# Applying the layer norms on ScalarE instead of VectorE, with new order tables, in a one-core macaron block

## The chip, the cores and the metric

The kernel runs on one core of a Trainium2 chip. The metric is device time in microseconds (us) for the whole program, from the first to the last instruction and what lies around them. The engines of a core each run their own queue of instructions in order and meet at semaphores: TensorE (PE, with its weight loads shown apart as PEld), VectorE (DVE), ScalarE (ACT), GpSimd (POOL) and SyncE (SP), which here issues every DMA.

## What is computed

The input is x of shape (8, 1024, 256), float32. A feed-forward step at half weight, an attention step and the same feed-forward step again are added to x, each on a layer norm of x:

```python
def _layernorm(x, axis=-1, eps=1e-05):
    m = jnp.mean(x, axis=axis, keepdims=True)
    v = jnp.var(x, axis=axis, keepdims=True)
    return (x - m) / jnp.sqrt(v + eps)

x = L0_attn_x
x = x + 0.5 * _L0_ffn_ref(_layernorm(x, axis=-1), ...)
x = x + _L0_attn_ref(_layernorm(x, axis=-1), ...)
x = x + 0.5 * _L0_ffn_ref(_layernorm(x, axis=-1), ...)
```

The feed-forward step is a 256x256 matrix with a bias, and eight low-rank experts of rank 16, of which each row takes the two with the largest gates. The attention step has 16 heads with causal softmax; keys and values come from a latent of 64 that is normed by its root mean square, queries from a latent of 128, and 32 of a head's 48 key and query columns are rotated.

## The kernel before, in words

Attention is worked in 32 quads: a quad g is four heads of one of the eight batches, so four quads make a batch. The work beside attention is cut into 32 jobs of 512 rows (four tiles of 128 rows by 256 columns): 16 jobs before attention (first feed-forward step, second layer norm, latents) and 16 after it (output projection, feed-forward step). Nearly all jobs run one after the other in lane 0, whose rows lie in the tile xa and whose normed rows lie in xn; job 1 and the last job run in lane 1, whose tiles are cut out of the tile probs and so bear that name in the trace.

The order of every engine's steps is written out by hand as a table of letters, ORDER: a head, a stretch for one batch that is repeated four times, and a tail. Each letter stands for the next step of one kind. On TensorE, S is one score tile (two matmuls, lines 643 and 645, into one of two banks of st_b), X one tile for the row maxima (line 673, into one of two banks of mx_b), V the probabilities times the values (line 661), P a projection (lines 694 to 700), T and F turns of keys and queries and of the maxima (lines 712, 679), J and j a piece of a job. On ScalarE, E is the exponential of a score tile (line 733), C and H copies for P and T (lines 742, 743, 755). On VectorE, M is a row maximum (lines 820 and 823), L the second half of a turn (line 864). Because each engine takes its queue strictly in that order, a step that is not ready holds up all that stands behind it.

A layer norm goes like this. VectorE takes the statistics of the four tiles (line 885) and joins them into mean and variance, mv (line 892). GpSimd adds the epsilon to the variance (line 1026, into ve) and raises it to the power -0.5 (line 1028, into rs). VectorE then makes xn of xa, four instructions of 128x256 a layer norm in two steps of two (line 906), and the semaphore normed lets TensorE transpose xn (line 587) and GpSimd add the bias to xa (line 1035). A job before attention has two layer norms and a job after attention has one: 48 layer norms, 192 instructions of line 906.

Behind that, TensorE's job pieces are named tr0, tr1 (transposes, line 587), low0, low1 (line 594), gated_tr (599), y0, y1 (605, 607), tr20, tr21 (587), qc (613), kv (619), kvt (625) and, for a job after attention, first wo0 and wo1 (line 576), the output projection. wo0 needs the tile aoc, a load of 512 KB of the attention's results (line 507). It stands in SyncE's queue behind the load of the job's rows xa (line 491), which in turn stands behind the store of the job before (line 513) or, when that job was one before attention, behind the store of its latents (lines 519, 520). Those wait for the copy out of kvt.

The row maxima go back into the scores as an extra row: after the turn F (line 679) VectorE writes the tile shift (line 838), SyncE stores it to DRAM (539) and loads it back as a row of st (543), and the first score of that half of the quad waits for it.

## Time and profile before

| what | us |
|---|---|
| median of 3 runs | 2131.92 |
| lowest and highest of the 3 | 2131.22, 2135.18 |
| the profiled execution | 2139.53 |
| its span, first to last instruction | 2137.8 |

Busy times of the profiled execution over its span: PE 2013.1 us (94%), DVE 1675.6 (78%), ACT 1263.9 (59%), POOL 972.0 (45%); the mean granted clock of TensorE is 0.985 of full speed. In the profile a matmul's end is modelled, so TensorE can be shown as busy while it in fact waits for a short time between two matmuls: the distance from one start to the next says more than the duration. Idle time shown for an engine is attributed to what released it.

### The profile page before, as it was taken

How to read it: one execution, taken by the hardware profiler on the slowest of the kernel's cores; microseconds unless marked ns; L12 is line 12 of the kernel's file. 1: busy time of each engine (PE TensorE's matmuls, PEld its weight loads, DVE VectorE, ACT ScalarE, POOL GpSimd, SP SyncE). 2: the span in 40 equal slices, each digit the busy share in tenths (PEclk: the TensorE clock that was granted, in tenths of full speed). 3: DMA queues.
4: the chain of work that ended last, by engine and by line, in shares of the span. 5: the costliest groups of instructions: out<-in, count | busy, mean ns of one | idle time of the engine just before them, and what ended most of it. 6: DMA issues, size and time to landing. Idle time of an engine off the chain costs nothing.

```text
span 2137.8 us, 38517 instructions
## 1 busy us (share of the span) xinstructions
PE 2013.1 (94%) x13248; PEld 1559.8 (73%) x13248; DVE 1675.6 (78%) x4924; ACT 1263.9 (59%) x2857; POOL 972.0 (45%) x1574
## 2 busy tenths in 40 slices
PE   4799999999999999999999999999999999999995
PEld 3677777777777777777777777777777777777754
DVE  4698888777888788888888878887788877888842
ACT  4456676655665566666566555665666655665750
POOL 5543544544545544344544435452444544444511
PEclk9999999999999999999999999999999999999997
DMA  2131221223112222213212232123221222212111
GB/s 75 45 75 31 80 54 46 61 70 95 44 43 73 73 80 56 59 45 90 81 41 70 68 79 57 41 70 80 85 56 46 58 86 82 65 51 56 36 31 42
DMA packets 71666, 132.34 MB, mean 62 GB/s; under 512 B 9840, under 2 KB 28528, under 8 KB 71472
## 3 DMA queue, kind: packets, MB, share of 16 engines
q1 hardware_dynamic: 71472, 129.87, 22.7%
q8 instruction: 107, 1.75, 0.3%
q14 instruction: 87, 0.71, 0.1%
HBM read 40.97 MB, written 38.54 MB: 37 GB/s over the span
## 4 chain that ended last, share of the span: by engine, by line
PE 71%; DVE 17%; DMA 4%; issue 3%; ACT 2%; POOL 1%; SPq 1%; POOLq 0%; DVEq 0%; ACTq 0%
PE mx_b L673 11%; PE st_b L643 11%; PE st_b L645 10%; PE o_b L661 9%; PE wj_b L605 5%; DVE st L864 4%; PE tp_b L712 3%; DVE mx_b L820 3%; PE wp_b L697 3%; PE wj_b L576 3%; PE wj_b L607 2%; PE wp_b L694 2%; DVE xn L906 2%; DMA aoc<-ao_scratch 2%; PE wj_b L594 2%
## 5 line engine op out<-in xcount | busy, mean ns | idle before, releaser
L733 ACT ACTIVATE probs<-st_b 128x512 f32<-128x512 f32 (+3 forms) x1536 | 699.2, 490 | 516.9 <-PE st_b L645 500.7
L820 DVE CUSTOM_DVE_ANT_0 mx_b<-mx_b,tri 128x256 f32<-128x256 f32 (+3 forms) x1024 | 513.7, 511 | 79.8 <-PE mx_b L673 72.5
L643 PE MATMUL st_b<-st 113*128 113x512 f32 (+2 forms) x1536 | 566.1, 373 | 8.6 <-DMA st<-shift_scratch 6.4
L673 PE MATMUL mx_b<-st 112*128 112x256 f32 (+2 forms) x1536 | 540.3, 387 | 16.9 <-DVE mx_s L820 14.6
L645 PE MATMUL st_b<-st,k_st 112*128 112x512 f32 (+2 forms) x1536 | 530.4, 350 | 0.0
L1012 POOL TENSOR_TENSOR rot_c<-qk,cos_s 128x256 f32<-128x256 f32 x256 | 191.6, 748 | 590.2 <-ACT v_s L743 589.5
L823 DVE TENSOR_REDUCE mx_s<-mx_b 128x1 f32<-128x512 f32 (+1 forms) x512 | 334.4, 653 | 91.0 <-PE mx_b L673 87.0
L864 DVE TENSOR_TENSOR st<-tp_b,st 48x512 fp32r<-48x512 f32 x512 | 352.4, 688 | 44.3 <-ACT st L755 30.9
L673 PEld LDWEIGHTS mx_b<-st 112*128 112x128 f32 x1536 | 275.7, 190 | 131.6 <-issue 58.4
L755 ACT ACTIVATE st<-tp_b 48x512 fp32r<-48x512 f32 x512 | 302.8, 591 | 74.6 <-PE tp_b L712 63.5
L643 PEld LDWEIGHTS st_b<-st 113*128 113x128 f32 x1536 | 292.9, 191 | 55.6 <-ACT probs L733 14.1
L645 PEld LDWEIGHTS st_b<-st,k_st 112*128 112x128 f32 x1536 | 294.1, 191 | 22.3
L1000 POOL TENSOR_SCALAR_AFFINE_SELECT probs<-probs 128x512 f32<-128x512 f32 x256 | 163.5, 639 | 294.4 <-ACT probs L733 293.8
L661 PE MATMUL o_b<-probs,v_s 128*17 128x512 f32 (+3 forms) x3072 | 285.6, 489 | 2.5 <-POOL probs L1000 2.5
L1017 POOL TENSOR_TENSOR qk<-rot_c,rot_s 128x256 f32<-128x256 f32 x256 | 189.1, 739 | 20.1
L661 PEld LDWEIGHTS o_b<-probs,v_s 128*17 128x17 f32 x3072 | 70.6, 97 | 144.8 <-issue 116.8
L742 ACT ACTIVATE qk<-wp_b 128x384 f32<-128x384 f32 x256 | 125.9, 492 | 71.1 <-PE wp_b L700 66.2
L712 PE MATMUL tp_b<-ident,qk 128*112 128x128 f32 x1024 | 154.3, 272 | 4.9 <-DVE shift L838 3.4
L697 PE MATMUL wp_b<-wkr_s,cur 128*128 128x128 f32 x1024 | 155.6, 274 | 0.0
L697 PEld LDWEIGHTS wp_b<-wkr_s,cur 128*128 128x128 f32 x1024 | 147.5, 191 | 0.0
L820 DVE DVE_READ_ACCUMULATOR2_ANT mx_s<- 128x1 f32 x1024 | 138.8, 136 | 1.6
L712 PEld LDWEIGHTS tp_b<-ident,qk 128*112 128x112 f32 x1024 | 120.3, 133 | 23.5 <-issue 7.2
(151 smaller groups left out, 2553.4 us busy)
## 6 DMA issues: line engine op xcount, KB each, us to landing
k_st<-st SPq DMA_DIRECT2D x128, 384.0 KB, 6.1
nx_scratch<-stg SPq DMA_DIRECT2D x14, 768.0 KB, 3.5
cur<-nx_scratch SPq DMA_DIRECT2D x14, 768.0 KB, 4.4
ao_scratch<-o_f SPq DMA_DIRECT2D x256, 32.0 KB, 1.7
xa<-in_x SPq DMA_DIRECT2D x15, 512.0 KB, 4.6
x_scratch<-xa SPq DMA_DIRECT2D x15, 512.0 KB, 2.8
xa<-x_scratch SPq DMA_DIRECT2D x15, 512.0 KB, 3.3
aoc<-ao_scratch SPq DMA_DIRECT2D x15, 512.0 KB, 4.3
```

What stands on the lines that cost most here:

```text
L643: nc.tensor.matmul(dst, k1_st[u][0:SHIFT + 1, a, P * j:P * j + P], q_st[u][0:SHIFT + 1, a, q0:q0 + w], start=True, stop=False)
L645: nc.tensor.matmul(dst, k2_st[u][0:SHIFT, a, P * j:P * j + P], q_st[u][0:SHIFT, a, q0:q0 + w], start=False, stop=True).then_inc(st_full, 1)
L661: last = nc.tensor.matmul(o_b[32 * a:32 * a + DV + 1, 0, q0 - HALF * h2:q0 - HALF * h2 + n], v_s[q][:, j, a, :], probs[:, a, PLACE[s]:PLAC ...
L673: nc.tensor.matmul(mx_b[:, m % 2, 0:w], q_st[u][0:SHIFT, a, P * i:P * i + P], k1_st[u][0:SHIFT, a, k0:k0 + w], start=True, stop=True).then ...
L697: nc.tensor.matmul(wp[:, HQ:2 * HQ, DC:DQ], cur[:, k, kk * P:(kk + 1) * P], wkr_s[:, kk, q, :].rearrange("p (a c) -> p a c", c=DR), start= ...
L712: last = nc.tensor.transpose(tp_b[0:TURN, 0, P * c:P * c + P], flat[:, P * c:P * c + TURN], ident[:, :])
L733: nc.scalar.activation(probs[:, a, PLACE[s]:PLACE[s] + n], st_b[:, a % 2, HALF - n:HALF], ACT.Exp, scale=SCALE).then_inc(exp_done, 1)
L755: nc.scalar.activation(heads(st[g % 2][rows], e, k), tp_b[rows, 0, :].rearrange("p (s y n) -> p s y n", s=2, n=P), ACT.Copy).then_inc(hi_d ...
L820: nc.vector.tensor_tensor_reduce(src, src, tri[:, HALF - n:HALF], 1.0, NEG, ALU.add, ALU.max, dst).then_inc(mx_done, 1)
L823: nc.vector.tensor_reduce(dst, src, AX_X, ALU.max).then_inc(mx_done, 1)
L864: last = nc.vector.tensor_tensor(heads(st[g % 2][other], e, k), tp_b[rows, 0, :].rearrange("p (s y n) -> p s y n", s=2, n=P), heads(f32(st ...
L1012: nc.gpsimd.tensor_tensor(rot_cos, d[:, :, DC:DQ], cs, ALU.mult)
```

## The change

The last step of a layer norm moves from VectorE to ScalarE. There it is an ACTIVATE with the function Identity, whose scale is rs and whose bias is a new column nb, both one value a row. GpSimd makes nb: it negates the mean into nm, and after rs multiplies nm by rs. VectorE's subtract and multiply (line 906) goes away. The order tables of all five engines are written anew; heads and tails change in length by some steps, the repeated stretch holds the same steps on TensorE, GpSimd and SyncE, twelve fewer on VectorE and twelve more on ScalarE.

```diff
-FFN_DVE = [("stats", 0, 0), ("stats", 0, 1), ("aggr", 0), ("norm", 0, 0), ("norm", 0, 1)]
+FFN_DVE = [("stats", 0, 0), ("stats", 0, 1), ("aggr", 0)]
...
-LAT_DVE = [("stats", 1, 0), ("stats", 1, 1), ("aggr", 1), ("norm", 1, 0), ("norm", 1, 1), ("ss",), ("kvn",)]
+LAT_DVE = [("stats", 1, 0), ("stats", 1, 1), ("aggr", 1), ("ss",), ("kvn",)]
...
-FFN_ACT = [("evac", "tr0"), ("evac", "tr1"), ("evac", "low0"), ("evac", "low1"), ("ex",), ("evac", "gated_tr")]
-LAT_ACT = [("evac", name) for name in LAT_MM]
+FFN_ACT = [("norm", 0, 0), ("norm", 0, 1), ("evac", "tr0"), ("evac", "tr1"), ("evac", "low0"), ("evac", "low1"), ("ex",), ("evac", "gated_tr")]
+LAT_ACT = [("norm", 1, 0), ("norm", 1, 1)] + [("evac", name) for name in LAT_MM]
...
+                self.nm, self.nb = take("nm" + tag, [P, GT]), take("nb" + tag, [P, GT])
...
+                elif name == "norm":
+                    own = lanes[LANE[g]]
+                    k, part = arg
+                    if part == 0:
+                        act.wait_ge(own.rstd[k], count(g, k) + 1)
+                    for tk in range(2 * part, 2 * part + 2):
+                        last = nc.scalar.activation(own.xn[:, tk, :], own.xa[:, tk, :], ACT.Identity,
+                                                    bias=own.nb[:, tk:tk + 1], scale=own.rs[:, tk:tk + 1])
+                    if part:
+                        last.then_inc(own.normed[k], 1)
...
-                elif name == "norm":
-                    k, part = arg
-                    if part == 0:
-                        dve.wait_ge(own.rstd[k], count(g, k) + 1)
-                    for tk in range(2 * part, 2 * part + 2):
-                        last = nc.vector.tensor_scalar(own.xn[:, tk, :], own.xa[:, tk, :], own.mv[:, tk, 0:1], own.rs[:, tk:tk + 1],
-                                                       ALU.subtract, ALU.mult)
-                    if part:
-                        last.then_inc(own.normed[k], 1)
...
-                    pool.wait_ge(own.rv[k], n + 1)
-                    nc.gpsimd.tensor_tensor(own.rs[:, :], own.ve[:, :], powers[:, :], ALU.pow).then_inc(own.rstd[k], 1)
+                    nc.gpsimd.tensor_scalar(own.nm[:, :], own.mv[:, :, 0], -1.0, None, ALU.mult)
+                    pool.wait_ge(own.rv[k], 2 * n + 1)
+                    nc.gpsimd.tensor_tensor(own.rs[:, :], own.ve[:, :], powers[:, :], ALU.pow).then_inc(own.rv[k], 1)
+                    pool.wait_ge(own.rv[k], 2 * n + 2)
+                    nc.gpsimd.tensor_tensor(own.nb[:, :], own.nm[:, :], own.rs[:, :], ALU.mult).then_inc(own.rstd[k], 1)
```

Of the tables two lines are enough to see their form, the start of SyncE's repeated stretch:

```diff
-        "assakJssJJkasskaJssJJJkcasskassJJJckasskaJssJk",
+        "ssakJssaJJksaskaJssJJJkcasskcassJJJkasskJJsask",
```

What the tables move is seen at three places. The first is TensorE's queue between kvt of a job before attention and wo0 of the job after it (tile aoc), in the repeated stretch; wj_b is the bank of lane 0. Before, the last twelve rows up to wo0 are these, and ahead of them stand, back to kvt, the rows of one V, one P, one T, four S of 256 and six X:

```order
L643 MATMUL st_b<-st 128x256
L645 MATMUL st_b<-st,k_st 128x256
L643 MATMUL st_b<-st 128x256
L645 MATMUL st_b<-st,k_st 128x256
L712 MATMUL tp_b<-ident,qk 112x128 x4
L673 MATMUL mx_b<-st 128x384
L643 MATMUL st_b<-st 128x256
L645 MATMUL st_b<-st,k_st 128x256
L643 MATMUL st_b<-st 128x256
L645 MATMUL st_b<-st,k_st 128x256
L673 MATMUL mx_b<-st 128x512
L576 MATMUL wj_b<-wo_s,aoc 128x256 x4
```

In the changed kernel the last twelve rows are these:

```order
L673 MATMUL mx_b<-st 128x512
L712 MATMUL tp_b<-ident,qk 112x128 x4
L673 MATMUL mx_b<-st 128x512
L643 MATMUL st_b<-st 128x512
L645 MATMUL st_b<-st,k_st 128x512
L673 MATMUL mx_b<-st 128x512
L643 MATMUL st_b<-st 128x512
L645 MATMUL st_b<-st,k_st 128x512
L694 MATMUL wp_b<-wq_s,cur 128x4x48
L697 MATMUL wp_b<-wkr_s,cur 128x4x32 x2
L700 MATMUL wp_b<-wkv_s,kvc 128x4x2x16
L576 MATMUL wj_b<-wo_s,aoc 128x256 x4
```

Between the V and wo0 there were four S of 256, four X and a T before; now there are four S of 512, five X, a T and a P. Between kvt and the V stands six S of 256 in place of four, and the other steps are the same kinds.

The second place is the second layer norm of the second job of the repeated stretch (job 13). On VectorE before, between the row maxima (mx_s) and the turns (st):

```order
L838 TENSOR_SCALAR shift<-tp_b 16x128
L823 TENSOR_REDUCE mx_s<-mx_b 128x1
L820 ISA mx_b,mx_s<-mx_b,tri 128x256
L820 ISA mx_s 128x1
L823 TENSOR_REDUCE mx_s<-mx_b 128x1
L906 TENSOR_SCALAR xn<-xa,mv,rs 128x256 x4
L820 ISA mx_b,mx_s<-mx_b,tri 128x256
L820 ISA mx_s 128x1
```

On ScalarE in the changed kernel, the same layer norm stands between exponentials (probs):

```order
L755 ACTIVATE st<-tp_b 48x4x128 x2
L733 ACTIVATE probs<-st_b 128x512 x2
L742 ACTIVATE qk<-wp_b 128x8x48
L743 ACTIVATE v_s<-wp_b 128x4x16
L768 ACTIVATE xn<-xa,nb,rs 128x256 x4
L733 ACTIVATE probs<-st_b 128x512 x2
L805 ACTIVATE stg<-wj_b 128x2x256
```

The four instructions left the queue of the row maxima and joined that of the exponentials.

The third place is SyncE's queue where a job after attention is followed by one before attention. Before:

```order
L513 DMA out_y<-xa 128x4x256
L539 DMA shift_scratch<-shift 16x128
L543 DMA st<-shift_scratch 1x4x512
L491 DMA xa<-in_x 128x4x256
L532 DMA k_st<-st 48x4x512
```

In the changed kernel:

```order
L513 DMA out_y<-xa 128x4x256
L491 DMA xa<-in_x 128x4x256
L539 DMA shift_scratch<-shift 16x128
L551 DMA ao_scratch<-o_f 16x512 x4
L543 DMA st<-shift_scratch 1x4x512
```

The load of xa, which waits until the store of out_y has landed, moved ahead of the store of shift.

## Rows read from the trace of the kernel before

**Rows 1.** The page: busy time, share of the span and instructions of each engine.

```profile
PE 2013.1 (94%) x13248; PEld 1559.8 (73%) x13248; DVE 1675.6 (78%) x4924; ACT 1263.9 (59%) x2857; POOL 972.0 (45%) x1574
```

**Rows 2.** Stretches: span, busy (x instructions) of PE PEld DVE ACT POOL, clock, DMA.

```profile
1245.50:1504.10 258.60, 248.01 (x1658) 194.67 (x1657) 209.00 (x615) 155.60 (x357) 119.26 (x195) 0.99 0.24 65
1440.00:1500.00 60.00, 54.24 (x329) 42.01 (x322) 43.82 (x126) 30.80 (x66) 18.23 (x30) 0.94 0.27 71
```

**Rows 3.** Waits of TensorE: us in total, times, longest.

```profile
PE wj_b L587 <- DVE xn L906: 31.4, 16, 23.6
PE wj_b L576 <- DMA aoc<-ao_scratch: 18.4, 6, 4.7
PE mx_b L673 <- DVE mx_s L820: 14.6, 28, 1.0
```

**Rows 4.** TensorE around two wo0: start us, us, instruction, [idle before].

```profile
1476.99 0.64 PE L625 MATMUL wj_b<-ident,kvn 128*96 128x128 f32 x4
...
1484.74 0.39 PE L673 MATMUL mx_b<-st 112*128 112x512 f32 x1
1489.88 3.75 PE L576 MATMUL wj_b<-wo_s,aoc 128*128 128x256 f32 x8 [4.74 <-DMA aoc<-ao_scratch]
...
1745.60 1.97 PE L576 MATMUL wj_b<-wo_s,aoc 128*128 128x256 f32 x8 [2.15 <-DMA aoc<-ao_scratch]
```

**Rows 5.** SyncE at the first of these places.

```profile
1478.28 0.34 SPq L519 DMA_DIRECT2D nx_scratch<-stg  x1
...
1480.59 0.43 SPq L507 DMA_DIRECT2D aoc<-ao_scratch  x1
```

**Rows 6.** Groups by line: xcount | busy us, mean ns | idle before.

```profile
L906 DVE TENSOR_SCALAR xn<-xa,mv,rs 128x256 f32<-128x256 f32 x180 | 88.4, 544 | 14.5 <-POOL rs L1028 14.0
...
L795 ACT ACTIVATE xt<-wj_b 128x512 f32<-128x512 f32 x60 | 35.9, 599 | 31.3 <-PE wj_b L587 30.8
...
L1026 POOL TENSOR_SCALAR ve<-mv 128x4 f32<-128x4 f32 x45 | 10.3, 228 | 59.4 <-DVE mv L892 59.3
...
L791 ACT ACTIVATE kvt<-wj_b 128x256 f32<-128x256 f32 x15 | 5.8, 385 | 7.8 <-PE wj_b L619 7.8
```

**Rows 7.** Timeline of SyncE and TensorE behind a job after attention.

```profile
1533.36 0.40 SPq L513 DMA_DIRECT2D out_y<-xa  x1
...
1536.74 0.38 SPq L507 DMA_DIRECT2D aoc<-ao_scratch  x1
...
1545.77 1.46 PE L576 MATMUL wj_b<-wo_s,aoc 128*128 128x256 f32 x6
```

**Rows 8.** TensorE where little waits: P, then X, S and S.

```profile
1006.67 0.49 PE L694 MATMUL wp_b<-wq_s,cur 128*128 128x192 f32 x2
...
1007.58 0.48 PE L673 MATMUL mx_b<-st 112*128 112x512 f32 x1
1007.90 0.39 PE L643 MATMUL st_b<-st 113*128 113x512 f32 x1
...
1008.36 0.40 PE L643 MATMUL st_b<-st 113*128 113x512 f32 x1
```

**Rows 9.** Waits, all engines: us in total, times, longest.

```profile
ACT probs L733 <- PE st_b L645: 500.7, 346, 8.0
...
PEld mx_b L673 <- DVE mx_s L820: 28.6, 60, 1.1
...
PEld st_b L643 <- ACT probs L733: 14.1, 43, 0.8
```

**Rows 10.** Timeline of one shift: turn, store, load, first score.

```profile
1250.67 0.27 PE L679 MATMUL tp_b<-ident,mxf 128*72 128x128 f32 x1
...
1252.00 0.36 SPq L539 DMA_DIRECT2D shift_scratch<-shift  x1
...
1255.24 0.66 SPq L543 DMA_DIRECT2D st<-shift_scratch  x1
...
1257.34 0.50 PE L643 MATMUL st_b<-st 113*128 113x512 f32 x1 [1.43 <-DMA st<-shift_scratch]
```

More of the change, by code:

```diff
@@ new lines @@
+        "FSXXSTXSXSXPSXXSTSXXSVXXSSTXXSSPXXSSPXXSSJXSSXVXSSXPSSXXSSXVSSXTSXSJXSXSPXSSXTSJXSXSVFXXSSTXSXPXXJSSXXTS"
+        "SXVXSSXTSXSXPSXSXVXSFXSXTXSSXXPXSXSPXSXSTXXSSVXXSSTXSXSPXXSSVXSXSPXSSXJSSXXJSSXXTSSXVSSXXTSSXPSSXJFSXSXV"
+        "XSXSTSXSXPXXSSVXSXSJXSXSTXSXSJXPSSJFXXSSXTXSXSXJXXSSXPXSXSXVXXJTSXSXPSSVXXSSTXSXSPXSXSVXSSXTSSXPSSXXPSSX"
+        "JSXSXJSXTSJXSSVJFSXXSPSSTXXVXSXSPXSXSXTXSXSVXSJXSXSJXSXSJFSSPSTSPSSVXXSSXJXTSXXJSXSXPJXXSSJXXTSSXPXSXSVX"
+        "XJSSXTXSSXPXSSXVXXSSXTXSXSPJXSXSJXSXSTSXSVSSPSSTXPXSXSJVJFXXPJXXTVJSXSXTSXSPXXSSPXSXSTSXSXVJXXSSFJXXSSJX"
@@ new lines @@
+        "XSSTXSXSXPXSXSTXSXSXVXXSSJXXSSTJXXSSPXSXSVXSXSPSXSXVSXSXJSXSXJSSXJXSSTJSSPFXXSSVXXSSTXXSSPXXSSJXXSSXTXSS"
+        "JXXSSJXXSSTVSSPSFXXSPXXSSTVXXPSXXSTXSXPXXSSVXXSSTXSXSJPXXSSJXSSXTSX",
+        "SXSXJXSXSJXXSSTXSXSVXXSSPXSXSVSFXXSPXXSSTVXXSSXTXSSXPJXXSSJXXSSJXXSSTVSSPFXXSSPXXSSTXSSXVJXXTSXJXSSXJXXS"
+        "SJXXSSPXXSSVJXXSSTXSSXPXSSXPXSXSXTXSSXVXSSPXSXSTXVJSSPJFXXSSPJXXSSTJXXSVXSXSTSXSXVXXSSPSJXXSSJXXSSJFSSPT"
+        "SSVXXSSXJXTSXXJSSPXXJXXSSJXXTSSXPXSXSVXXJSSXTXSSXPXSSXVXXSSXTXSXSPJXSXSJXSXSTSXSVSSPSSTXPXSXSJVJFXXPJXXT"
@@ new lines @@
+        "VJSXSXTSXSPXXSSPXSXSTSXSXVJXXSSFJXXSSJXXSSTXSXSXPXSXSTXSXSXVXXSSJXXSSTJXXSSPXSXSVXSXSPSXSXVSXSXJSXSXJSSX"
+        "JXSSTJSSPFXXSSVXXSSTXXSSPXXSSJXXSSXTXSSJXXSSJXXSSTVSSPSFXXSPXXSSTVXXPSXXSTXSXPXXSSVXXSSTXSXSJPXXSSJXSSXT"
+        "SX",
+        "SXSXJXSXSJXXSSTXSXSVXXSSPXSXSVSFXXSPXXSSTVXXSSXTXSSXPJXXSSJXXSSJXXSSTVSSPFXXSSPXXSSTXSSXVJXXTSXJXSSXJXXS"
+        "SJXXSSPXXSSVJXXSSTXSSXPXSSXPXSXSXTXSSXVXSSPXSXSTXVJSSPJFXXSSPJXXSSTJXXSVXSXSTSXSXVXXSSPSJXXSSJXXSSJFSSPT"
+        "SSVXXSSXJXTSXXJSSPXXJXXSSJXXTSSXPXSXSVXXJSSXTXSSXPXSSXVXXSSXTXSXSPJXSXSJXSXSTSXSVSSPSSTXPXSXSJVJFXXPJXXT"
@@ new lines @@
+        "VJSXSXTSXSPXXSSPXSXSTSXSXVJXXSSFJXXSSJXXSSTXSXSXPXSXSTXSXSXVXXSSJXXSSTJXXSSPXSXSVXSXSPSXSXVSXSXJSXSXJSSX"
+        "JXSSTJSSPFXXSSVXXSSTXXSSPXXSSJXXSSXTXSSJXXSSJXXSSTVSSPSFXXSPXXSSXTXVXXTPXXSSJXXSSTPXXSSVXXSSJXXSSTPXXSSV"
+        "XXSSPXXSSVXXSSJXSSXJXSSJXXSSTJXSSPXSSXTXSSVXXFPXXTVXXPSSXXTSSXXPSSXJSXSXJFSXSXJXSXSTXSXSXVXXSSXTXSXSPXXS"
+        "SJXXSSTPXXSSVXXSSJXSXSTSPXSSXVSSXSXPSXSXTSXJSXSXVJSXSPJFSSXXJSXXSTXSSXVSXSXSXTSXSXPXSSVXXSSTPJXXSSJFXXSS"
+        "JXXSSTXSXSXPXSSXVXXTPXXSSXPXSXSVXXSSTXSXSPXSXSVXSSXTSSXXSSXPSSXTSXSXVSXSXPSSXXTPSSXXVSXFSXPSSXXTXVXSSXTS"
@@ new lines @@
+        "HEEJECEJEEJEEHHEECEJEEHEHECEEEEHHEECEEHHEEEECEEHHCEEEEEHHCJJEEHHEECEEHHEECEEEEHEHECEEHEHEEEEECEECEEJEEEE"
+        "EEHHEEEEHEHECEEJEEHEHCEEJEEHEHCJEEHHEEEEHHEECEEJEEHHEECEECEEHHEEEEEECEEEECEEJEEHHEEHHEEEEHEEHCEEEEEEHEEH"
+        "JCEEJEEJEEHHEEJCEEJEEHHEEJEECEEJHEEHCEEEEHEHECEEEEEEHHCEEJJEEJECEJEHEHJEEJEECJEEHHEECEEHHEEEJEEEEEECEHEH"
+        "CEEJJEEJHEHJEECJEEJHEEHCEEJEEHEHECEEEEHHEECEEEEHEEHEECEEJJHEEHJCJJHHCJEEHHJEECEEEEHEHECJEEEEEEHEHECEEHEH"
+        "EEEEEEECEEEEHHJEEJCEEJEEJEEJEEHHJEECEEJEEHHEECEEJEEHHEEEEEEHHEECEECHHEECEJEHEHJEECEEHEHEJCEEJEEE",
@@ new lines @@
+        "HEHEJEEJEEHHEEEEJCEEEECEEHHEEHHEECJEEEEEEHHEECEECEEHHJJEEJHEJEEHJEEJEECEEJEEHEHECEECEEHHEEEECJJEEHHJEECJ"
+        "EEJEEHHJCEJEEHEEHEECEJEEEEEEHHEECJJEEJHEHJEECJEEJHEEHCEEJEEHEHECEEEEHHEECEEEEHEEHEECEEJJHEEHJCJJHHCJEEHH"
+        "JEECEEEEHEHECJEEEEEEHEHECEEHEHEEEEEEECEEEEHHJEEJCEEJEEJEEJEEHHJEECEEJEEHHEECEEJEEHHEEEEEEHHEECEECHHEECEJ"
+        "EHEHJEECEEHEHEJCEEJEEE",
+        "HEHEJEEJEEHHEEEEJCEEEECEEHHEEHHEECJEEEEEEHHEECEECEEHHJJEEJHEJEEHJEEJEECEEJEEHEHECEECEEHHEEEECJJEEHHJEECJ"
+        "EEJEEHHJCEJEEHEEHEECEJEEEEEEHHEECJJEEJHEHJEECJEEJHEEHCEEJEEHEHECEEEEHHEECEEEEHEEHEECEEJJHEEHJCJJHHCJEEHH"
@@ new lines @@
+        "MMLLMMoMMooMMoMMfLLJJnMMJJJJJMMJJJMMLLMMMMMMLLJMMJMMfoLLoonMMoJMMJLLJMMMMMMLMMLMMMMLLMMMM",
+        "MMLMLMMMMJMMLLJMMJJJMMfJonMMoJoMoMJLLMMJJMMLMLMMJMMJMMJfLLJonMMoJoMoMMLMLMMMMLMLMMMMJMMJMMMLMLMMMMMMJJLJ"
+        "LMMMMMofLLoonMMoMMLMJMJJJLJMJMJMJMJLJMMLooMMooJMMfJnJJJLLMMMMLMMLMMMMMMJMLMMLJMMMMLMLMMMMMMLLMJMMJMJJLJL"
+        "MMofMooMMoLLnMMMMLLoJMJJMJMJLJMJMJLMJMJMMoLfoLMMonJMMJMMMMLMLMMMMMLLMMJMMJMMJMMJJMMLLMMoMMooMMoMMfLLJJnM"
+        "MJJJJJMMJJJMMLLMMMMMMLLJMMJMMfoLLoonMMoJMMJLLJMMMMMMLMMLMMMMLLMMMM",
```

106 lines of the change are left out of this document (34 added, 72 removed).

## The prediction, made before the changed kernel was run

> **What bounds the kernel now.** I read the busy shares first [rows 1]: TensorE is busy 94% of the span, VectorE 78%, ScalarE 59%, GpSimd 45%. In one period of the repeated stretch TensorE is busy 248 of 258.6 us, VectorE 209 and ScalarE 156 [rows 2]. So TensorE's queue is the bound, and a saving on VectorE is worth only what TensorE waits for it. The second view is what TensorE waits for [rows 3]. The largest wait but one is wj_b L576 for the tile aoc, 18.4 us in six times, all in the middle of the program. The largest, wj_b L587 for xn, is 31.4 us in 16 times, but one of these is the 23.6 us at the very start, where the program fills; the other 15 make 7.8 us. Waits for a row maximum (mx_s) are 14.6 us. The third view is the timeline around one of these six, the one with the longest wait [rows 4, 5]. kvt starts at 1476.99, the last matmul ahead of wo0 at 1484.74, and wo0 only at 1489.88. SyncE issues the store of the latents at 1478.28, then the load of xa, then that of aoc at 1480.59; it lands 9.3 us later. The store can't go before kvt is done, so wo0 comes some 12 us behind kvt here whatever stands between, and the rows between fill 7.8 us. The eight records of this wo0 took 3.75 us, those of the last of the six, after a wait of 2.15 us, 1.97 us: after the long wait TensorE ran at half its clock for a while, 1.2 in place of 2.4 GHz, and the granted clock of the 60 us around it is 0.94 [rows 2].
>
> TensorE also loses time that isn't shown as idle. Its weight loads waited 28.6 us for row maxima of line 820 and 14.1 us for exponentials [rows 9]. These are short waits, a matmul that starts some 0.1 to 0.3 us after it could.
>
> **The change, part by part.**
>
> *VectorE loses line 906.* It is 180 instructions in lane 0, 88.4 us [rows 6], and 12 more at about 0.4 us: some 93 us, 5.6% of VectorE's busy time. It is off TensorE's queue. What TensorE waits for VectorE's row maxima is 14.6 + 28.6 = 43 us [rows 3, 9]. If it falls by the share by which VectorE's work falls, 2.4 us are gained; if each of the 48 layer norms delays one maximum by half of its own four instructions' time (4 x 0.54 us), all of the 43 us are. I take 4 us, since most of these waits are those of two X in a row with two banks, which a layer norm elsewhere in the queue doesn't touch. The price of nothing at all is the other end.
>
> *ScalarE gains 192 ACTIVATEs of 128x256.* The trace has no such ACTIVATE with a scale and a bias from a tile. The nearest row is the copy kvt, the same size, 385 ns; a row of twice the size, xt, has 599 ns [rows 6]. So 74 us at the low end and 115 us at the high end, for ScalarE 62 to 65% busy. In a row they overlap a little; four take some 1.3 to 2.2 us. Four of line 906 took 2.2 us at the mean of 544 ns, so the copy itself gets no longer. What it costs TensorE: the exponentials behind it come later by its length, and there are two banks of scores. A score takes 0.46 us of TensorE [rows 8], two of them 0.92. Where scores follow at once, TensorE waits for the difference, 0.4 to 1.3 us; where X, P or V stand between, nothing. Over 48 layer norms that is between 0 and 62 us. TensorE's weight loads wait 14 us for exponentials in 43 times, while ScalarE waits 500.7 us for scores [rows 9], so ScalarE usually has caught up. I take 5 us.
>
> The Trainium skill, "ScalarE: Activation LUTs", section "What ACT_TABLE_LOAD costs", speaks against the change: an ACTIVATE with immediate operands takes 186 ns + 0.833 ns an element, and each operand read from a tile adds 93 ns. For 256 columns and two such operands that is an estimate of 585 ns each and 112 us in all. By it the same part would cost TensorE some 10 us more than I take. No row here shows such an instruction; the copies of 256 columns at 385 ns agree with the page's form without such operands (399 ns).
>
> *GpSimd gains two instructions a layer norm.* ve is 228 ns on four columns [rows 6]; nm and nb are of its size, so 48 x 0.46 = 22 us of an engine that is busy 45%. nm lies beside the wait for ve, nb on the chain to xn: 0.3 to 0.5 us later. Where the layer norm is the chain of the program (twice at the start, twice at the end) this shows: +1 us.
>
> *The order at wo0.* This is the largest term. Counted with the prices of [rows 8] (a P is 0.91 us from its first matmul to the next step, an S of 512 is 0.46, an S of 256 half of it, an X of 512 a quarter of a microsecond), the changed queue has between kvt and wo0, against the one before, four S that are 512 wide and not 256 (+0.9), one X (+0.2), one P (+0.9), two S of 256 (+0.5) and slightly narrower X (-0.1): 2.4 us more. The stores and loads on SyncE stand in the same order behind kvt. So each wait should be 2.4 us shorter. Six waits are 18.4 us [rows 3], of which the largest is 4.7 and the smallest, 2.15, is in [rows 4]; six times 2.4 is 14.4, so some 4 us are left and 14 are gained. With the waits the low clock goes. The slow wo0 of [rows 4] took 1.8 us longer than the other; for a clock that goes with each wait near 3 us or more, of which the mean of 3.1 us allows about three, I take 4 us, at the worst none. Together -18 us; between -5, if the load of aoc lands as much later as it is wanted later, and -24.
>
> *The same for the second job after attention.* There the distance from y1 of the job before to wo0 shrinks by the same count from 12.8 to 9.7 us. The store goes out at 1533.36, the load of aoc at 1536.74, wo0 runs at 1545.77 [rows 7]. The load's own time isn't seen, since nothing waits for it: it is under 9.0 us, and 9.3 us where it shared the queues with the store of the latents [rows 4, 5]. If it takes half of that, 4.6 us, the tile is there 4.4 us early, and 3.1 us less leaves 1.3; it is hidden by the P, S and X between. If it takes 7 us, it costs 1 us six times. I take +1.
>
> *The shift.* The way from turn to first score is long: in [rows 10] the turn starts at 1250.67, the store goes at 1252.00, the load at 1255.24, and the score starts at 1257.34 having waited 1.43 us. That is 6.7 us with a store that waited 3 us; with half of that wait it is some 5 us. Before, the steps between turn and score of the second half last 6.9, 6.0, 5.0 and 4.8 us in the four quads of a period, now 4.7, 7.1, 4.4 and 4.0, counted as above. The two last come 0.6 to 0.8 us short where they just did before, the first is met without a queue ahead of it. Half a microsecond to one a period and quad, over 8 periods: +5 us, between 0 and 15. The xa load moved ahead of a shift on SyncE (third place in the section on the change) makes SyncE wait some 3 us for the store to land; the first-half shift behind it has about 19 us until its score, so nothing is seen of it.
>
> *The rest of the order.* TensorE does the same steps; two X in a row occur 402 times against 360, each pair costs some 0.1 us, +4; fewer steps stand between S or X and a V at a bad seam, -3. Call it +1.
>
> Sum: -18 - 4 + 5 + 1 + 1 + 5 + 1 = -9, and with rounding -10 us on the profiled execution's 2139.5. That execution is 7.6 us above the median of 2131.92. The difference I take over unchanged: 2122 us.
>
> **The rivals.**
>
> *VectorE was more of a bound than it looks.* For it: VectorE is 81% busy in the repeated period and TensorE's waits for its maxima are 43 us; against it: VectorE itself waits for row maxima from TensorE. Then half of the 43 us goes and the gain at wo0 comes too: -22 - 18, with 13 us of the other costs against it, -27: 2105.
>
> *The gain at wo0 is given back.* For it: six loads and stores are in flight when aoc is fetched, and the new distances at the shift and at the second wo0 are shorter. Then -18 is met by +15 at the shift, the second wo0 and the exponentials: 2130, no change.
>
> *ScalarE's queue holds up the scores (slower).* Each block of four in front of exponentials with two banks. It decides from the point where four ACTIVATEs take longer than two scores, 0.92 us, and no other work stands between on TensorE. At 2.0 us a block, 1.1 us is lost in each of the 48 places: +52, so in place of the +5 of the sum 2169. In half of the places it is +26: 2143. With a quarter, +13, it is within the forecast's reach again, 2130; 2143 is the case I weigh. For it speaks the high end of the price; against it ScalarE's 500 us of waiting for scores [rows 9]. The Trainium skill's rule in the same page, section "Rules for kernel authors", to keep multiply and add on VectorE, is this rival.
>
> **How the numbers follow.** Forecast, -4 to -18 us: 0.43. VectorE rival: 0.15. Given back, within 4 us: 0.20. ScalarE rival, or the shift at its worst: 0.22. A measurement of this kernel can tell 0.2%, some 4 us, from no change. So faster 0.58, same 0.20, slower 0.22. The range from 2102 to 2145 leaves out the far end of the first and of the last rival.
>
> **What would show it.** Right: TensorE's wait for aoc at L576 falls from 18.4 to some 5 us, and the wo0 records are near 1.9 us; line 906 is gone from VectorE and its busy time is near 1583; the ACTIVATEs of xn are near 0.4 to 0.6 us each and ScalarE's busy time is 1340 to 1380; TensorE's waits at L643 for st<-shift_scratch rise by some 5 us. Wrong: the waits of TensorE's weight loads for probs at L643 rise from 14.1 us above 40; or the wait for aoc stays near 18; or a new wait at tr20 (L587 for xn, now from ScalarE) above 10 us in the middle; then the norm is late on ScalarE's queue.

## The result, and the profile after

| | us |
|---|---|
| the changed kernel, median of 4 runs (lowest, highest) | 2101.64 (2100.80, 2103.88) |
| the kernel before, on the same chip | 2131.57 |
| ratio, with its 95% interval | 0.9862 (0.9842 to 0.9882) |
| the same two in two later sets of runs | 0.9833 (0.9804 to 0.9863), 0.9835 (0.9808 to 0.9861) |

The changed kernel is faster by 29 to 36 us, where I had forecast 10. It came out 20 us under the predicted time and just under the range. The direction was right, and two of the terms were far off.

First the page after, busy time, share and instructions of each engine, beside [rows 1], and its fourth part, the chain of work that ended last, by engine:

```profile
PE 2004.3 (95%) x13248; PEld 1558.0 (74%) x13248; DVE 1600.8 (76%) x4732; ACT 1346.8 (64%) x3049; POOL 989.7 (47%) x1670
PE 79%; ACT 9%; DVE 5%; issue 3%; DMA 2%; POOL 2%; SPq 0%; POOLq 0%; ACTq 0%; DVEq 0%
```

The same part of the page of before, a row that I had not used:

```profile
PE 71%; DVE 17%; DMA 4%; issue 3%; ACT 2%; POOL 1%; SPq 1%; POOLq 0%; DVEq 0%; ACTq 0%
```

By busy time VectorE goes from 78% to 76%, which looks like nothing. On the chain (the work that ended last, followed back step by step to what released it) it goes from 17% of the span to 5%, and ScalarE from 2% to 9%. That is the move seen in one view.

The waits of TensorE and of its weight loads after, beside [rows 3] and [rows 9] (us in total, times, longest):

```profile
PE wj_b L587 <- ACT xn L768: 36.1, 26, 24.5
...
PE mx_b L673 <- DVE mx_s L830: 7.1, 15, 1.5
...
PE wj_b L576 <- DMA aoc<-ao_scratch: 3.6, 3, 1.7
```

```profile
PEld st_b L643 <- ACT probs L733: 22.3, 67, 0.9
PEld mx_b L673 <- DVE mx_s L830: 13.2, 36, 0.9
PEld mx_b L673 <- DVE mx_s L833: 9.6, 26, 0.9
```

The weight loads' waits for the other line of row maxima, 823 (833 after), were not among the rows that I had used. Before they were:

```profile
PEld mx_b L673 <- DVE mx_s L823: 17.5, 44, 0.6
```

The wait for aoc is nearly gone (18.4 to 3.6 us). The waits for the maxima, now line 830, have halved (14.6 to 7.1, and for the weight loads 28.6 to 13.2 and 17.5 to 9.6). The waits for exponentials grew from 14.1 to 22.3. The wait for xn, now made by ScalarE, is 11.6 us in 25 times beside the one of 24.5 at the start; before it was 7.8 in 15.

One period of the repeated stretch, and the 60 us with a wo0 in them, beside [rows 2]; then this wo0 and SyncE's load for it, beside [rows 4, 5]; and the new group of line 768, beside [rows 6]:

```profile
1334.90:1583.30 248.40, 244.66 (x1658) 192.94 (x1658) 199.72 (x590) 165.96 (x381) 121.67 (x207) 1.00 0.25 67
```

```profile
1440.00:1500.00 60.00, 58.86 (x417) 46.60 (x415) 48.25 (x142) 40.88 (x96) 32.41 (x54) 1.00 0.34 93
```

```profile
1466.09 1.97 PE L576 MATMUL wj_b<-wo_s,aoc 128*128 128x256 f32 x8 [0.79 <-DMA aoc<-ao_scratch]
```

```profile
1458.13 0.44 SPq L507 DMA_DIRECT2D aoc<-ao_scratch  x1
```

```profile
L768 ACT ACTIVATE xn<-xa,nb,rs 128x256 f32<-128x256 f32 x180 | 95.0, 595 | 24.4 <-POOL nb L1032 23.7
```

The period fell from 258.6 to 248.4 us with the same 1658 matmuls. The load of aoc lands 7.8 us after its issue, and TensorE now reaches wo0 0.8 us ahead of it, where before it was 4.7 us ahead; the granted clock is 1.00 in both stretches, so TensorE stays at 2.4 GHz. Between 200 and 2000 us the changed kernel's trace has no time at 1.2 GHz. The trace of before has 20.5 us of it there, in five places, four of them at a wo0 that waited for aoc. At half speed that is worth 10 us at most.

### The profile page after: what moved, and what is told of

Same layout as the page of the kernel before. It is cut to its first block, busy times and chain, and to the rows that moved or that the text cites. A ratio compares the mean times of both kernels' runs of the same rounds, so it can differ in the third digit from the quotient of the medians.

```text
span 2102.2 us, 38613 instructions
## 1 busy us (share of the span) xinstructions
PE 2004.3 (95%) x13248; PEld 1558.0 (74%) x13248; DVE 1600.8 (76%) x4732; ACT 1346.8 (64%) x3049; POOL 989.7 (47%) x1670
## 3 DMA queue, kind: packets, MB, share of 16 engines
q1 hardware_dynamic: 71472, 129.87, 23.2%
## 4 chain that ended last, share of the span: by engine, by line
PE 79%; ACT 9%; DVE 5%; issue 3%; DMA 2%; POOL 2%; SPq 0%; POOLq 0%; ACTq 0%; DVEq 0%
PE mx_b L673 13%; PE st_b L643 12%; PE st_b L645 11%; PE o_b L661 10%; PE wj_b L605 5%; PE wp_b L697 4%; PE tp_b L712 4%; PE wp_b L694 3%; ACT xn L768 3%; PE wj_b L576 3%; PE wj_b L607 3%; ACT probs L733 2%; PE wp_b L700 2%; PE wj_b L594 2%; PE wj_b L587 2%
## 5 line engine op out<-in xcount | busy, mean ns | idle before, releaser
L643 PE MATMUL st_b<-st 113*128 113x512 f32 (+2 forms) x1536 | 558.3, 368 | 7.8 <-ACT probs L733 5.0
L643 PEld LDWEIGHTS st_b<-st 113*128 113x128 f32 x1536 | 291.8, 190 | 58.3 <-ACT probs L733 22.3
L645 PEld LDWEIGHTS st_b<-st,k_st 112*128 112x128 f32 x1536 | 293.7, 191 | 23.7
```

The costliest lines, as they stand in the source:

```text
L643: nc.tensor.matmul(dst, k1_st[u][0:SHIFT + 1, a, P * j:P * j + P], q_st[u][0:SHIFT + 1, a, q0:q0 + w], start=True, stop=False)
L645: nc.tensor.matmul(dst, k2_st[u][0:SHIFT, a, P * j:P * j + P], q_st[u][0:SHIFT, a, q0:q0 + w], start=False, stop=True).then_inc(st_full, 1)
```

## The experiments

Ratios are to the kernel before on the same chip, with 95% intervals. An edit that adds or takes lines shifts the line numbers of its rows, by up to 49 lines; the names of the tiles stay, so xn, mx_s and aoc are found by them.

### The load of aoc: e1, e4, e7

e1 is the kernel before with SyncE's stream of job steps rearranged, so that the load of aoc stands ahead of the store of the latents and of the load of xa. Its tables are unchanged.

```diff
+def aoc_first(steps):
+    for i in range(len(steps) - 1):
+        if steps[i][0] == "nx_store" and steps[i + 2][0] == "ao_load":
+            steps[i:i + 3] = [steps[i + 2], steps[i], steps[i + 1]]
+    return steps
```

> The kernel before, with one step of SyncE moved: the load of aoc for a job after attention that follows one before attention is issued ahead of the store of the latents and the load of xa, not behind them. Nothing else changes. If the six waits of wo0 for aoc (18.4 us) and the low clock behind them are worth what the prediction's term says, the wait disappears and the time falls by 18 to 22 us, to some 2111. If TensorE would have met another wait there anyway, it falls by under 8 us.

Measured: 2109.97 us, 0.9888 (0.9857 to 0.9918), 24 us less. The wait for aoc is gone from the trace and the other waits stand as they were (maxima 14.2 us, shift 7.3). The gain is more than the listed 18.4 us; the low clock went with the waits, for e1's trace has no time at 1.2 GHz between 200 and 2000 us.

e4 is the changed kernel with wo0 set forward in TensorE's table in six places, which takes 2.4 us of steps from between kvt and wo0.

```diff
-XSXSPJ
+JXSXSP
```

> The changed kernel with wo0 put back ahead of one P, two S of 512 and two X, some 2.3 us of TensorE's work, in the six places where it waited for aoc in the kernel before. If the distance to the load is what counts, the wait for aoc returns to 14 to 18 us and the time is 2114 to 2120. If not, it stays within 4 us of 2101.6.

Measured: 2123.09 us, 0.9945 (0.9929 to 0.9961), some 21 us more than the changed kernel (18 to 24 by the ratios), and the wait is back. Below it stands one of its wo0 that ran at half clock:

```profile
PE wj_b L618 <- DMA aoc<-ao_scratch: 14.9, 7, 3.3
```

```profile
470.31 3.65 PE L618 MATMUL wj_b<-wo_s,aoc 128*128 128x256 f32 x8 [1.75 <-DMA aoc<-ao_scratch]
```

So the distance is what counts, and 2.4 us in six places are worth about 21 us; removing the wait altogether (e1) is worth 24. The listed wait is 11 us of the one (3.6 to 14.9) and 18 us of the other. A part of the rest can be the clock: e4's trace has 10.2 us at 1.2 GHz between 200 and 2000 us, worth 5 us at most.

e7 is the changed kernel with the edit of e1.

> The changed kernel with the one further edit of e1: SyncE issues the load of aoc ahead of the store of the job before and of the load of xa, for jobs after attention. In the changed kernel TensorE waits 3.6 us for aoc in three times. Theory A (nearly all of the aoc term is already gained by the new order): 3 to 6 us below the changed kernel, 2096 to 2099 (ratio to before 0.983 to 0.985), the wait for aoc is gone and no other wait changes by over 2 us. Rival B (the xa load, now second, is late for the copy or the earlier load pushes the shift's store and load back): 0 to +10 us, 2101 to 2112, with a longer wait for shift_scratch at L643 or for xn at L587.

Measured: 2099.31 us, 0.9817 (0.9798 to 0.9836). The last 3.6 us of the wait are gone; against the changed kernel's 2101.6 to 2102.7 that is 2 to 3 us, which these runs don't tell from none.

### Each half of the change alone: e2, e3

e2 has the layer norms on ScalarE in the order of before. The norm steps were taken out of VectorE's table and put into ScalarE's at the place that TensorE's queue had reached where VectorE's stood. e3 is the reverse, VectorE's layer norms in the new order.

```diff
-LAT_DVE = [("stats", 1, 0), ("stats", 1, 1), ("aggr", 1), ("norm", 1, 0), ("norm", 1, 1), ("ss",), ("kvn",)]
+LAT_DVE = [("stats", 1, 0), ("stats", 1, 1), ("aggr", 1), ("ss",), ("kvn",)]
...
-LAT_ACT = [("evac", name) for name in LAT_MM]
+LAT_ACT = [("norm", 1, 0), ("norm", 1, 1)] + [("evac", name) for name in LAT_MM]
```

> The layer norms on ScalarE, but in the order tables of the kernel before; a norm stands in ScalarE's queue where the work ahead of it is as far along as it was on VectorE. Theory 1 (the new order makes the gain): no gain, 2125 to 2140, with the wait for aoc still near 18 us. Theory 2 (relief of VectorE makes the gain beside wo0): TensorE's waits for row maxima fall by half and the time falls by 10 to 15 us, to some 2118.

> The reverse: the layer norms on VectorE as before, in the new order tables. Theory 1 (the order makes the gain): 2101 to 2110. Theory 2 (VectorE's relief makes a third to a half of it): 2112 to 2122, with TensorE's waits for row maxima near those of the kernel before.

Measured: e2 2213.75 us, 1.0373 (1.0341 to 1.0406); e3 2154.73 us, 1.0095 (1.0064 to 1.0126). Both are slower than either whole kernel. In e2 ScalarE comes to its norm before nb is there, and the exponentials stand behind it; in e3 VectorE comes to its norm before rs is there, and the maxima stand behind it. First e2, then e3:

```profile
PE st_b L685 <- ACT probs L775: 38.9, 38, 6.2
...
ACT xn L810 <- POOL nb L1074: 48.6, 31, 7.5
```

```profile
PE mx_b L714 <- DVE mx_s L861: 38.3, 39, 4.3
...
DVE xn L947 <- POOL rs L1069: 18.0, 18, 5.1
```

The changed kernel has 23.7 us in place of these 48.6. This shows that a norm at a place that was made for another engine costs more than the move brings. It doesn't show that the order of before has no good place for it: one way of placing was tried.

### What the layer norms cost on either engine: e5, e6, f2

These three leave out most of the normalisation. Each step of a layer norm in lane 0 makes one piece of 128x32 in place of two of 128x256, and the rest of xn is zero. All other steps, waits and tables stay. e5 is before, e6 the changed kernel, f2 is e5 with the early load of e1.

```diff
-                    for tk in range(2 * part, 2 * part + 2):
-                        last = nc.vector.tensor_scalar(own.xn[:, tk, :], own.xa[:, tk, :], own.mv[:, tk, 0:1], own.rs[:, tk:tk + 1],
+                    for tk in range(2 * part, 2 * part + 1):
+                        last = nc.vector.tensor_scalar(own.xn[:, tk, 0:32], own.xa[:, tk, 0:32], own.mv[:, tk, 0:1], own.rs[:, tk:tk + 1],
```

> The kernel before, its order tables unchanged; each VectorE step of a layer norm makes one 128x32 piece in place of two of 128x256 (the rest of xn is zero), so most of the normalisation is left out, and VectorE is relieved of some 75 to 80 us without any other engine getting more to do. Theory A (my prediction's term: the saving on VectorE is worth little, the gain is in the order): 2127 us, 4 us below before (ratio 0.998, between 0.995 and 1.000); TensorE's waits for maxima stay within 3 us of 14.6, and those of its weight loads within 5 us of 28.6. Rival B (VectorE was more of a bound than its 78% shows): 10 to 20 us below before, 2112 to 2122 (ratio 0.991 to 0.995), and the weight loads' waits for maxima halve, as they did in the changed kernel (28.6 to 13.2 us).

> The changed kernel, its order tables unchanged; each ScalarE step of a layer norm makes one 128x32 piece in place of two of 128x256 (most of the normalisation is left out), so ScalarE is relieved of some 85 to 95 us. It measures what the layer norms on ScalarE cost where they now stand. Theory A (the order hides them, ScalarE waits 413 us for scores anyway): 2097 us, up to 6 us below the changed kernel's 2101.6; the waits of TensorE's weight loads for probs at L643 (22.3 us) fall by 5 to 8 us. Rival B (they cost the 10 to 15 us that the price of 595 ns an instruction suggests): 2087 to 2092 us. The ratio to the kernel before would be 0.984 for A and 0.979 to 0.981 for B.

> The kernel before with both single edits at once: VectorE's layer norm steps of one 128x32 piece (as in e5, most of the normalisation left out) and SyncE's early load of aoc (as in e1). Theory A (the two gains are of different places and add up: ratios 0.9858 and 0.9888): 0.9746, 54 us below before, 2084 us, as fast as the changed kernel with small layer norms (e6, 0.9755), so that nothing of the rest of the new order is needed to explain the time. Rival B (they overlap, since a TensorE that doesn't wait for aoc waits for maxima instead): 0.980 to 0.984, 35 to 43 us below before, and then the new order has a further gain of its own of 10 to 20 us.

Measured: e5 2107.71 us, 0.9858 (0.9841 to 0.9875), 30 us less; e6 2086.46 us, 0.9755 (0.9734 to 0.9776); f2 2087.92 us, 0.9764 (0.9736 to 0.9791). Busy times and chain of e5, then its waits:

```profile
PE 1995.2 (95%) x13248; PEld 1554.4 (74%) x13248; DVE 1627.1 (77%) x4830; ACT 1260.9 (60%) x2857; POOL 969.8 (46%) x1574
PE 77%; DVE 11%; DMA 4%; issue 3%; ACT 2%; POOL 1%; SPq 1%; POOLq 0%; DVEq 0%; ACTq 0%
```

```profile
PE wj_b L628 <- DVE xn L948: 24.9, 1, 24.9
PE wj_b L617 <- DMA aoc<-ao_scratch: 17.2, 6, 4.4
PE mx_b L714 <- DVE mx_s L862: 11.0, 19, 1.0
```

This is the run that broke my first term. 48.5 us of VectorE's time, with nothing put elsewhere and with the wait for aoc still there, were worth 30 us. And f2, which has only the early load beside it, is as fast as e6, which has the whole new order: beyond the distance at aoc and the load on VectorE, the new tables bring no more than these runs can tell (2 us). The two kernels differ in one thing more, though. In f2 the small layer norms are still on VectorE (busy 1626.2 us), in e6 they are on ScalarE (VectorE 1602.1), so the 2 us are the tables, 24 us less on VectorE and the cost of small norms on ScalarE together, and no run parts them.

### Way to xn, or time of the engine: f3, f4, g2

A layer norm on VectorE can cost in two ways: TensorE waits for xn itself, and the row maxima queued behind come later. f3 is e5 (most of the normalisation left out) with filler instructions behind the signal that xn is ready. They delay what is queued, but not xn.

```diff
                     if part:
                         last.then_inc(own.normed[k], 1)
+                        for q in range(3):
+                            nc.vector.tensor_scalar(junk[:, q, :], ident[:, 0:20], 1.0, 0.5, ALU.subtract, ALU.mult)
```

f4 is the changed kernel with four such instructions behind each joining of the statistics. g2 is e6 with eight small ACTIVATEs behind ScalarE's signal.

> As e5 (VectorE's layer norm steps of one 128x32 piece, most of the normalisation left out), but behind the second of them, when TensorE already has the signal that xn is ready, VectorE has three further instructions of 128x20 to a tile that nobody reads: some 48 x 3 x 0.44 = 63 us of busy time, so VectorE is as busy as before, or by some 10 us more. Theory A (what counts is VectorE's time as such, for it holds up the row maxima behind): the 30 us of e5 are lost again, ratio 0.996 to 1.003. Rival B (what counts is the way from statistics to xn, which e5 shortened by 1.3 us a layer norm): the time stays near e5, ratio 0.985 to 0.989.

> The changed kernel, in which VectorE has four further instructions of 128x20 behind the joining of the statistics of each layer norm, to a tile that nobody reads: 192 instructions, some 80 us of busy time, as many instructions as the layer norms took from it. ScalarE and the orders stay. Theory A (VectorE's relief is worth some 30 us of time for 48 us of busy time, as e5 shows): the changed kernel loses 30 to 50 us, ratio 1.000 to 1.010, and TensorE's waits for maxima go back to 40 us and more. Rival B (the new order has slack for it): 0 to 8 us, ratio 0.986 to 0.990.

> As e6 (the changed kernel with ScalarE's layer norm steps of one 128x32 piece, most of the normalisation left out), but behind the second of them, when TensorE has the signal that xn is ready, ScalarE has eight further ACTIVATEs of 128x5 to a tile that nobody reads, some 8 x 0.2 = 1.6 us a layer norm, as much as the smaller steps saved; ScalarE is as busy as in the changed kernel. Theory A (what the layer norms cost on ScalarE is the way to xn, which TensorE waits for at the first transpose): 2 to 5 us over e6, ratio 0.976 to 0.979. Rival B (it is ScalarE's time as such, which holds up the exponentials): the 15 us of e6 are lost again, ratio 0.982 to 0.986.

Measured: f3 2121.13 us, 0.9914 (0.9882 to 0.9946); f4 2107.32 us, 0.9850 (0.9822 to 0.9878), where the changed kernel beside it had 2102.69 and 0.9833; g2 2084.98 us, 0.9753 (0.9725 to 0.9781), where the changed kernel beside it had 2101.85 and 0.9835. The filling was smaller than I meant. The fillers' group in f3, then in g2 (those of f4 are like those of f3):

```profile
L955 DVE TENSOR_SCALAR junk<-ident 128x20 f32<-128x20 f32 x144 | 23.2, 218 | 0.0
```

```profile
L816 ACT ACTIVATE junk<-ident 128x5 f32<-128x5 f32 x360 | 39.2, 197 | 0.0
```

f3 gave VectorE back 20 of the 48.5 us (busy 1646.9) and lost 12 of e5's 30 us, with an interval of some 8 us either way. So VectorE's time as such is dear in the order of before, roughly 0.6 us of the program for one of VectorE, and the rest of the 30 us isn't proven to be the way to xn, since the filling was incomplete. In f4 18 us more of VectorE (1618.5 for 1600.6) cost some 4 us, within the intervals of none: the changed kernel has slack there. g2 gave ScalarE back 28 of the 59 us that e6 had saved and lost nothing that the intervals, some 7 us together, can tell. ScalarE's layer norms cost 17 us in the changed kernel (g2 against it, on one chip), and the half of ScalarE's time that was given back is not what costs them. For the other half that isn't shown.

### A signal for each half: g3, g4, g5, g6

TensorE's first transpose step (tr0, tr20) reads the first two tiles of xn, but waits for all four. With the whole computation kept, g3 (the changed kernel) and g4 (before) signal after each step of two tiles. g5 and g6 add the early load of aoc to them.

```diff
-                    if k == 0:
-                        pe.wait_ge(own.normed[second], count(n, second) + 1)
+                    pe.wait_ge(own.normed[second], 2 * count(n, second) + 1 + k)
...
-                    if part:
-                        last.then_inc(own.normed[k], 1)
+                    last.then_inc(own.normed[k], 1)
...
-                        pool.wait_ge(own.normed[0], IN_LANE[g] + 1)
+                        pool.wait_ge(own.normed[0], 2 * IN_LANE[g] + 2)
```

> The changed kernel with the whole normalisation, in which ScalarE signals xn after each of its two steps of a layer norm, so that TensorE's first transpose step (tr0, tr20), which reads the first two tiles only, waits for the first step alone; tr1 and tr21 wait for the second. It shortens the way to the first transpose by 2 x 0.6 = 1.2 us. Theory A (this way costs 12 to 15 us in the changed kernel): 5 to 12 us below the changed kernel, ratio to before 0.978 to 0.982, and TensorE's wait for xn in the middle of the program (36.1 - 24.5 = 11.6 us in 25 times) falls below 5 us. Rival B (it is ScalarE's time that costs): within 2 us of the changed kernel, ratio 0.983 to 0.987.

> The kernel before, whole, with one edit: VectorE signals xn after each of its two steps of a layer norm, so that TensorE's first transpose step waits for the first step alone (as g3, but on VectorE and in the order of before). It shortens the way to the first transpose by 2 x 0.54 = 1.1 us and takes nothing from VectorE. Theory A (of e5's 30 us some 12 to 18 are this way, by e5 against f3): 7 to 14 us below before, ratio 0.9935 to 0.997. Rival B (with VectorE as full as it is, the maxima take the time that is freed): within 4 us of before, ratio 0.998 to 1.002.

> The changed kernel with both further edits that hold promise, the whole computation kept: a signal after each half of a layer norm (as g3) and SyncE's load of aoc ahead of the store and the load of xa (as e7). Theory A: 8 to 15 us below the changed kernel, 2088 to 2095, ratio 0.976 to 0.980. Rival B (neither is on the path any more): within 3 us of it, ratio 0.982 to 0.987.

> The kernel before, whole, its layer norms on VectorE and its tables as they were, with the half signals of g4 and the early load of aoc of e1. Theory A (the two add up: 7 to 14 and 23 us): 30 to 37 us below before, ratio 0.983 to 0.986, as fast as the changed kernel, so that what the move to ScalarE brings over it is only the maxima no longer held up. Rival B (they don't add up, because VectorE bounds what follows): 23 us or less, ratio 0.989 or more.

Measured: g3 2093.32 us, 0.9802 (0.9777 to 0.9826), against the changed kernel's 2101.85 and 0.9835 on the same chip; g5 2092.55 us, 0.9794 (0.9770 to 0.9818); g4 2130.56 us, 0.9984 (0.9967 to 1.0002); g6 2108.15 us, 0.9879 (0.9854 to 0.9904), no faster than e1's 0.9888. The waits of g3, then those of g4 with its weight loads:

```profile
PE wj_b L586 <- ACT xn L767: 24.2, 2, 23.5
PE mx_b L672 <- DVE mx_s L828: 10.1, 18, 1.9
```

```profile
PE wj_b L586 <- DVE xn L905: 22.5, 1, 22.5
PE mx_b L672 <- DVE mx_s L819: 16.8, 29, 2.0
```

```profile
PEld mx_b L672 <- DVE mx_s L819: 30.2, 58, 2.5
PEld mx_b L672 <- DVE mx_s L822: 21.6, 50, 1.0
```

The same edit removes the wait for xn from both kernels, but for the one at the start. In the changed kernel 8.5 us of the time go with it. In the kernel before most of it comes back as waits for the maxima (before, 14.6 us for TensorE, and 28.6 and 17.5 us for the weight loads), and the time falls by 3 us or not at all: TensorE runs ahead and meets VectorE, which has no room there. That is the clearest sign of what bounded the kernel before. Even with both edits it stays some 15 us behind g5, which has the same edits (18 us by the ratios; they ran on different chips).

### SyncE's table alone: e9

e9 is the kernel before with SyncE's table taken from the changed kernel.

> The kernel before with SyncE's table alone taken from the changed kernel (in which the store and load of a shift stand ahead of job loads and stores more often); everything else, the layer norms on VectorE too, is as before. Theory A (TensorE's wait for the shift at L643 fell from 6.4 to 2.1 us because SyncE is not held by other issues): that wait falls to 2 to 3 us and the time by 3 to 8 us, 2123 to 2129 (ratio 0.996 to 0.9985); the aoc wait at L576 stays near 18 us, since its load stands as far behind kvt as before. Rival B (the shift's wait fell because the turn stands elsewhere in TensorE's queue, and SyncE's order suits only its own tables): the wait stays at 5 to 8 us or grows, 2131 to 2145 us (ratio 1.000 to 1.006).

Measured: 2208.98 us, 1.0340 (1.0317 to 1.0362). Each theory had half of it: the wait for the shift fell (6.4 to 2.9 us), but SyncE now stands at stores of the shift that VectorE, in the order of before, writes late (its waits there were 84.6 us before), and the loads of aoc stand behind them. Half of the 12 waits are those of the second job after attention, 10.2 to 10.7 us each, where before there was none:

```profile
PE wj_b L617 <- DMA aoc<-ao_scratch: 79.8, 12, 10.7
```

```profile
SPq L580 <- DVE shift L879: 321.8, 39, 20.8
```

The changed kernel itself was run twice more, in the sets of f2 to f4 and of g2, g3 and g5; its ratios stand in the first table.

## Why the prediction was off, step by step

To see where TensorE loses time that no wait lists, I took each of its steps in the traces, from its start to the start of the next, less the shortest usual distance of that pair of steps (the 8th percentile over all the traces). What is over, in us, by the kind of the later step:

| | maxima (X) | scores (S) | first piece of a job: tr | wo | turns (T) | others | all |
|---|---|---|---|---|---|---|---|
| before | 92.0 | 67.8 | 15.4 | 19.8 | 10.1 | 47.1 | 252.2 |
| e5, small norm on VectorE | 79.8 | 60.8 | 3.4 | 18.4 | 9.8 | 44.4 | 216.6 |
| f3, the same, filled | 87.5 | 69.4 | 3.4 | 17.4 | 8.5 | 47.8 | 234.0 |
| g4, before, half signals | 99.2 | 68.3 | 4.9 | 16.4 | 10.5 | 45.7 | 245.0 |
| after | 80.7 | 64.2 | 23.9 | 4.3 | 5.2 | 37.0 | 215.3 |
| e6, small norm on ScalarE | 81.4 | 60.1 | 3.8 | 5.8 | 5.0 | 41.9 | 198.0 |
| g3, after, half signals | 83.2 | 69.7 | 9.3 | 1.6 | 5.1 | 36.8 | 205.7 |

Two things lie in these numbers besides waiting. Time at the low clock counts as excess: between 200 and 2000 us the traces have 20.5 us at 1.2 GHz before and in g4, 17.1 in f3, 10.2 in e5, 3.4 in g3 and none in the others. And the profiled execution of before took 7.6 us more than its median, so differences to the first row are too large by up to that much. Between kernels with different tables the split by kind also depends on which pairs of steps occur.

*VectorE loses line 906: forecast -4, measured -30 for a part of it (e5).* This is the step that failed: that a saving on VectorE is worth only what TensorE is listed as waiting for its row maxima, and that most of these 43 us, being those of two X in a row, a layer norm elsewhere in the queue doesn't touch. The 43 us also left out 17.5 us for line 823. The table shows e5's gain in three places: 12 us at the maxima, 7 at the scores (the shift is a chain through VectorE too), 12 at the transposes. Some 5 us of the first two are steps at the low clock, of which e5's trace has less. The scores and transposes were not in my term at all. And the 7.8 us that I read as the waits for xn, and left where they were, were 15 us by the distances and went with the norm. The chain's 17% for VectorE was a sign that I hadn't read. It doesn't give the size: in proportion, 48.5 of VectorE's 1675.6 us would be some 10 us of the chain, and e5 gained 30. The rival "VectorE was more of a bound than it looks" was right, with 0.15 far too low a chance. That its 2105 is 3 us from the result is in part luck: it had 22 us for VectorE where e5 has 30, and 13 us of costs where the measured ones are 17.

*ScalarE gains 192 ACTIVATEs: forecast +5, measured +17 (g2 against the changed kernel).* The price was 595 ns each, the high end of my bounds. The Trainium skill, "ScalarE: Activation LUTs", section "What ACT_TABLE_LOAD costs", gave an estimate of 585 by its formula, and the trace agrees; my cheap end, from the copy kvt at 385, was the form without operands from a tile. But I had charged the wrong customer. I expected exponentials to be late; the waits of the weight loads for them rose by 8 us only, and a ScalarE half filled again costs nothing that can be told (g2). The table has it at the transposes, 23.9 against 3.8 in e6: what TensorE waits for is xn. I had written that the making of xn gets no longer, since four of line 906 take 2.2 us. That is four times the mean, and it leaves out that they overlap: four in a row took 1.37 us at the least and, with interruptions under 3 us, 1.91 us on the mean in the trace of before, 2.06 and 2.11 us on ScalarE, and nb comes on top. A new wait there above 10 us stood on my list as a sign of a wrong forecast, and it is there with 11.6. The slower rival, ScalarE's queue holding up the scores at 2143, is refuted.

So the move itself is worth about -30 + 17 = -13 us, where I had +2 with GpSimd's share (GpSimd's +1 no run tests). The rule of the Trainium skill, "ScalarE: Activation LUTs", section "Rules for kernel authors", to keep multiply and add on VectorE, gives the wrong answer here: the instruction is dearer on ScalarE (595 ns for 544 on the mean, 593 for 413 on the median), but its place is cheaper.

*The order at wo0: forecast -18, measured -24 alone (e1), -21 to put back (e4), and about -20 beside the lighter VectorE (f2 less e5).* The mechanism was right, with the wait down to 3.6 us (I said 5) and the eight records of wo0 at 1.97 us. The low clock, which I priced at 4 us, may be more of it: the 20.5 us cost up to 10. That it goes with waits near 3 us or more doesn't hold either: in e4 a wo0 behind a wait of 1.75 us took 3.65 us, in e5 one behind a wait of 2.91 us took 1.97. And between kvt and the twelve rows shown of the queue before stand seven X, not six; the difference to the changed queue, one X, is right.

*The shift, the second wo0, the rest of the order: forecast +5, +1 and +1, measured near 0 together.* e6 against f2 leaves 1 to 2 us for all that the tables do beside aoc, with the small norms on different engines. For the shift the sign was wrong: TensorE's wait for it fell from 6.4 to 2.1 us. I had counted shorter distances and missed that SyncE's table puts the shift's store ahead of the stores and loads that it waited behind; in e9 this table alone brings the wait to 2.9 us, though TensorE waits so long for aoc there that it is no clean test. No wait for a second wo0 appears.

The rival that the gain at wo0 is given back did not happen. In sum: -30 (VectorE), +17 (ScalarE), -20 (aoc) give -33, and the measured gain is 29 to 36. That they agree is no proof by itself: the steps from before to e5, to f2, to e6 and to the changed kernel add up by construction. What is shown is the size of each step. VectorE's busy time fell by 75 us where I said 93; 7 us of the difference are overlap, since only 81.4 of the 88.4 us of line 906 are covered by no other instruction of VectorE, and the rest I can't place, for the row maxima of 128x512 take the same 687 to 688 ns. What stays open is how e5's 30 us divide between the way to xn and VectorE's time, for f3 filled less than half of what was freed.

The best kernel of the study is g3 or g5, which these runs don't tell apart: 2093 us, some 9 us under the changed kernel on the same chip, with the whole computation.

## What to carry to other kernels

Read the chain's share of an engine beside its busy share. Here VectorE at 78% busy held 17% of the chain, and taking work from it gave 0.6 us for each us; the listed waits for its maxima told neither the size nor the place of the gain, more than half of which was at scores and transposes, much of it in short delays between matmuls that don't show as waits. When a step moves to another engine, ask apart who waits for its result and who stands behind it in the queue; a filler behind the signal, and an earlier signal, measure the two. Signal the part of a result that the next engine reads first: this was worth 9 us where the producer had slack behind it, and 3 us or nothing where it had none. Read the spread of an instruction's time beside its mean, as the next section shows.
